# The second layer norm taken apart in a gated cross-attention block

## What is computed

```python
x1 = x + tanh(g_xattn) * attention(layernorm(x), ctx)
out = x1 + tanh(g_ffn) * ffn(layernorm(x1))

# attention, one of 8 samples, C = 256 rows by D = 1024
t = Wt @ ctx ; p = Wp @ layernorm(x) ; g = Wg @ ctx
att = sum over a group of 32 rows of p * g          # 8 groups
y = Wz (grouped) @ (att * t)
y normed over its group, * gn_w + gn_b, + ctx

# ffn, per row s of x1 after its layer norm
scores = (h @ Wq.T) @ keys.T                        # 64 experts
gate = softmax over the 16 highest scores
z = h @ A_w.T                                       # 64 experts of rank 8
out = (z * gate) @ B_w.T * 2
```

## Time and profile before

| quantity | value |
|---|---|
| device time, median of 3 runs | 394.64 us (394.6 to 395.23) |
| span of the profiled execution | 392.9 us |
| PE busy | 367.8 us, 94% of the span |
| DVE busy | 293.8 us, 75% |
| ACT busy | 131.0 us, 33% |
| POOL busy | 96.8 us, 25% |

### The profile page before, as it was taken

How to read it: one execution, slowest core, us unless ns; L and a number is a source line. 1 busy time by engine, 2 the same in 40 slices (tenths; PEclk the granted TensorE clock), 3 DMA queues, 4 the chain that set the end, 5 groups by cost and what they waited for, 6 DMA issues and landing times.

```text
span 392.9 us, 5668 instructions
## 1 busy us (share of the span) xinstructions
PE 367.8 (94%) x2051; PEld 321.2 (82%) x2051; DVE 293.8 (75%) x729; ACT 131.0 (33%) x204; POOL 96.8 (25%) x73
## 2 busy tenths in 40 slices
PE   6998489999999989999899989999899989999996
PEld 5776479888898878888798878988798878988994
DVE  3867899459974899649985799739985699738742
ACT  4574435203542136113432036213342035321310
POOL 0172152205140152304240150402440150401000
PEclk9999789999999999999999999999999999999999
DMA  7648001401150020501141011501132011001102
GB/s 257 237 139 300 15 2 44 172 0 54 53 214 0 12 95 6 207 0 53 53 160 54 0 53 53 214 0 53 53 100 113 0 53 53 0 0 53 55 24 84
DMA packets 10665, 30.36 MB, mean 77 GB/s; under 512 B 1937, under 2 KB 2705, under 8 KB 10657
## 3 DMA queue, kind: packets, MB, share of 16 engines
q1 hardware_dynamic: 10544, 30.19, 20.5%
q10 hardware_dynamic: 112, 0.07, 0.1%
HBM read 21.86 MB, written 8.39 MB: 77 GB/s over the span
## 4 chain that ended last, share of the span: by engine, by line
PE 77%; DVE 7%; POOL 6%; ACT 4%; issue 2%; DMA 2%; SPq 1%; ACTq 0%; POOLq 0%; DVEq 0%
PE w_ps L829 32%; PE z_ps L884 19%; PE w_ps L905 18%; DVE ln_sb L651 5%; POOL c_lo L294 4%; PE t_ps L870 4%; DMA x_sb<-in_x 2%; ACT c_hi L366 2%; PE t_ps L895 2%; PE w_ps L884 2%; POOL w_rs L316 1%; ACT hT_hi L396 1%; PE t_ps L812 1%; DVE x_st L501 1%; ACT q_hi L371 0%
## 5 line engine op out<-in xcount | busy, mean ns | idle before, releaser
L884 PE MATMUL z_ps<-A_hi,hT_hi 128*128 128x288 f32 x240 | 53.4, 304 | 0.6 <-DVE hT_lo L557 0.6
L884 PE MATMUL z_ps<-A_hi,hT_lo 128*128 128x288 f32 x240 | 51.9, 298 | 0.0
L884 PE MATMUL z_ps<-A_lo,hT_hi 128*128 128x288 f32 x240 | 51.9, 298 | 0.0
L905 PE MATMUL w_ps<-B_hi,zT_hi 128*128 128x512 f32 x128 | 51.3, 400 | 0.0
L304 POOL TENSOR_TENSOR q_lo<-ln_sb,q_hi 128x1024 fp32r<-128x1024 f32 x16 | 38.1, 2404 | 53.5 <-ACT q_hi L371 53.5
L905 PE MATMUL w_ps<-B_lo,zT_hi 128*128 128x512 f32 x128 | 49.9, 390 | 0.0
L905 PE MATMUL w_ps<-B_hi,zT_lo 128*128 128x512 f32 x128 | 49.9, 390 | 0.0
L396 ACT ACTIVATE hT_hi<-t_ps 128x512 fp32r<-128x512 f32 x32 | 17.4, 591 | 78.0 <-PE t_ps L870 78.0
L884 PEld LDWEIGHTS z_ps<-A_hi,hT_hi 128*128 128x128 f32 x240 | 39.4, 192 | 1.6 <-DVE hT_lo L557 1.0
L294 POOL TENSOR_TENSOR c_lo<-c_sb,c_hi 128x1024 fp32r<-128x1024 f32 x14 | 33.3, 2381 | 28.9 <-ACT c_hi L366 28.9
L884 PEld LDWEIGHTS z_ps<-A_lo,hT_hi 128*128 128x128 f32 x240 | 39.2, 192 | 0.0
(11 more groups left out here) (131 smaller groups left out, 787.8 us busy)
## 6 DMA issues: line engine op xcount, KB each, us to landing
x_sb<-in_x SPq DMA_DIRECT2D x8, 1024.0 KB, 5.0
c_sb<-in_ctx SPq DMA_DIRECT2D x7, 1024.0 KB, 7.0
out_block<-o_sb SPq DMA_DIRECT2D x14, 512.0 KB, 2.6
res_sb<-in_L_ffn_B_w SPq DMA_DIRECT2D x3, 512.0 KB, 3.5
c_sb<-in_ctx SPq DMA_DIRECT2D x2, 512.0 KB, 5.9
stage<-in_L_ffn_A_w SPq DMA_DIRECT2D x2, 512.0 KB, 6.3
res_sb<-in_L_ffn_A_w SPq DMA_DIRECT2D x2, 512.0 KB, 9.9
out_block<-o_sb SPq DMA_DIRECT2D x4, 256.0 KB, 2.0
```

The lines of the kernel that those rows point to most:

```text
L884: last = pe.matmul(banks[i][:, 0:ZH], h[:, t, row], w[:, k, i * ZH:(i + 1) * ZH], start=(k == 0 and h is hT_hi and w is A_hi), stop=(k == ...
L905: last = pe.matmul(w_ps[k][:, :], z[:, t, row], w[:, j, cols], start=(j == 0 and z is zT_hi and w is B_hi), stop=(j == KN - 1 and z is zT_lo))
```

## The change

The layer norm is split into a centring and a scale, and they go to different places:

- DVE takes the statistics of `u` from PSUM (`u_statistics(t)`), and forms minus the mean, `neg_u`. ACT waits for it (`u_mean`) and adds it as it copies `u` out of PSUM.
- `xt` is also given mean zero: DVE's instruction writes the row's sum beside it (`xt_sum`), POOL forms `neg_xt` and adds it to both tiles (`xt_center`, three instructions on POOL). For the first sample ACT makes the sums by two copies.
- So `w = u*slope + xt` has mean zero as it stands. PE transposes it from `uw_sb` without a norm. `h_tile` and the statistics of w go; ACT squares each tile with a sum beside it (`w_square`), POOL adds eps and takes the power (`w_root`, two instructions on POOL for both tiles).
- The scale `w_rs` is applied to the scores (as they leave PSUM) and to the gate (`g_scale`, one small instruction more in each `gate`).
- The residual's shift is replaced by `kappa`, made from `u_dev`, `slope` and `kappa0`; `kappa0` needs `xt_mid`, POOL's end of `xt_center`, and stands in `group_deviation`.
- Orders: `hT(1)` moves from the middle of `z_product(0)` into `out_product(3)`, and `hT(0)` into `out_product(2)`. The passes with the low part of ctx come last in a product, so that `u_product_next` waits for `c_lo` only ahead of its fifth pass. On POOL `x_root` stands ahead of `ctx_low(1)`. On DVE `x_plus_ctx` follows `x_stats` at once.

```diff
             def load(b, n_prev):
-                sp.wait_ge(xt_done, n_prev)
+                sp.wait_ge(xt_summed, n_prev)
+                sp.wait_ge(q_done[T - 1], n_prev)
...
+            def xt_center(n):
+                pool.wait_ge(xt_summed, n)
+                pool.tensor_tensor(neg_xt[:, :], xt_sum[:, :], minus_mean[:, :], ALU.mult).then_inc(pool_step, 1)
+                pool.wait_ge(pool_step, 1)
+                for t in range(T):
+                    last = pool.tensor_scalar(xt_sb[:, t, :], xt_sb[:, t, :], 1.0, neg_xt[:, t:t + 1],
+                                              ALU.mult, ALU.add)
+                last.then_inc(xt_mid, 1)
+
+            def w_root(n):
+                pool.wait_ge(w_squared, T * n if isinstance(n, int) else pool_w_squared)
+                pool.tensor_tensor(w_ve[:, :], w_sq[:, :], eps[:, :], ALU.add).then_inc(pool_step, 1)
+                pool.wait_ge(pool_step, 2)
+                pool.tensor_tensor(w_rs[:, :], w_ve[:, :], minus_half[:, :], ALU.pow).then_inc(w_rstd, 1)
...
+            def w_square(t, n):
+                act.wait_ge(w_done[t], n)
+                act.wait_ge(p_done[USES - 1], n)
+                act.activation(q_hi[:, t, :], uw_sb[:, t, :], ACT.Square, scale=1.0 / math.sqrt(D),
+                               accum_out=w_sq[:, t:t + 1]).then_inc(w_squared, 1)
...
                 act.wait_ge(u_done[k], n)
-                act.activation(uw_sb[:, t, h * HALF:(h + 1) * HALF], w_ps[k][:, :], ACT.Copy).then_inc(u_copied[k], 1)
+                act.wait_ge(u_mean[t], n)
+                act.activation(uw_sb[:, t, h * HALF:(h + 1) * HALF], w_ps[k][:, :], ACT.Identity,
+                               bias=neg_u[:, t:t + 1]).then_inc(u_copied[k], 1)
...
             for k in range(USES):
-                u_copy(k, 1)
                 for n in groups_after_u(k):
                     prep(n)
+                if k % NH == NH - 1:
+                    for j in range(k - NH + 1, k + 1):
+                        u_copy(j, 1)
                 if k == 1:
                     query_hi(1)
...
+            act.wait_ge(xt_done, 1)
+            for t in range(T):
+                last = act.activation(hT_hi[:, t, :], xt_sb[:, t, :], ACT.Copy, accum_out=xt_sum[:, t:t + 1])
+            last.then_inc(xt_summed, 1)
             for n in range(n_late, len(PREP)):
                 prep(n)
...
+            def u_statistics(t, n):
+                for h in range(NH):
+                    k = NH * t + h
+                    dve.wait_ge(u_done[k], n)
+                    step(dve.bn_stats(u_st[:, t, 6 * h:6 * h + 6], w_ps[k][:, :]))
+                settle()
+                step(dve.bn_aggr(u_mv[:, t, :], u_st[:, t, :]))
+                settle()
+                dve.tensor_scalar(neg_u[:, t:t + 1], u_mv[:, t, 0:1], -1.0, None, ALU.mult).then_inc(u_mean[t], 1)
...
                 step(dve.tensor_tensor(att_var[:, T:2 * T], a2[:, :], u_mv[:, :, 1], ALU.add))
+                dve.wait_ge(xt_mid, n)
+                step(dve.tensor_tensor(kappa0[:, :], gnb_t[:, :], neg_xt[:, :], ALU.subtract))
...
             def ffn_and_next(n, m, n_dma, m_dma):
                 x_stats(m, m_dma)
-                hT_low(1, n)
+                x_plus_ctx(m, m_dma)
                 gate(0, n)
+                u_statistics(0, m)
                 query(m, n)
-                x_plus_ctx(m, m_dma)
-                u_statistics(m)
+                u_statistics(1, m)
                 zT_low(0, n)
...
-                passes = [(w, v, c) for c in range(T) for w, v in ((w_hi, v_hi), (w_hi, v_lo), (w_lo, v_hi))]
+                passes = [(w, v_hi, c) for c in range(T) for w in (w_hi, w_lo)] + [(w_hi, v_lo, c) for c in range(T)]
...
-                out_product(2, n)
-                pe.wait_ge(zT_lo_s[1], n)
-                hT(0, m)
+                out_product(2, n, lambda: hT(0, m))
                 pe.wait_ge(p_reduced[3], m)
-                out_product(3, n)
+                out_product(3, n, lambda: hT(1, m))
```

More of the change, by code:

```diff
@@ L111, in flamingo_block @@
         y_ve, y_rs = sb("y_ve", [P, T]), sb("y_rs", [P, T])
-        slope, shift = sb("slope", [P, T]), sb("shift", [P, T])
+        slope, kappa = sb("slope", [P, T]), sb("kappa", [P, T])
         sc, sc1, sc2 = sb("sc", [P, NE]), sb("sc1", [P, NE]), sb("sc2", [P, NE])
@@ L440, in ffn_and_next @@
                 residual(n)
-                hT_high(1, n)
                 exps(0, n)
+                act.wait_ge(hT_done[2 * T - 1], n)
                 act.wait_ge(res_done, n)
-                for k in range(USES):
+                for k in range(NH):
+                    u_copy(k, m)
+                query_hi(m)
+                for k in range(NH, USES):
                     u_copy(k, m)
                 zT_high(0, n)
-                query_hi(m)
                 exps(1, n)
@@ L452, in ffn_and_next @@
                         zT_high(1, n)
-                hT_high(0, m)
+                for t in range(T):
+                    w_square(t, m)
+                    hT_high(t, m)
             with act.Fori(0, NB - 1) as b:
@@ L639, in shifts, with w_tile @@
-            def shifts():
-                step(dve.tensor_tensor(shift[:, :], g_mean[:, :], slope[:, :], ALU.mult))
-                settle()
-                step(dve.tensor_tensor(shift[:, :], gnb_t[:, :], shift[:, :], ALU.subtract))
-            def h_tile(t, n):
-                dve.wait_ge(w_rstd[t], n)
-                dve.wait_ge(q_lo_s, n)
-                for h in range(NH):
-                    cols = slice(h * HALF, (h + 1) * HALF)
-                    dve.tensor_scalar(ln_sb[:, t, cols], uw_sb[:, t, cols], w_mv[:, t, 0:1], w_rs[:, t:t + 1],
-                                      ALU.subtract, ALU.mult).then_inc(h_done[NH * t + h], 1)
+            def w_tile(t, n):
+                for k in range(NH * t, NH * t + NH):
+                    dve.wait_ge(u_copied[k], n)
+                dve.scalar_tensor_tensor(uw_sb[:, t, :], uw_sb[:, t, :], slope[:, t:t + 1], xt_sb[:, t, :],
+                                         ALU.mult, ALU.add).then_inc(w_done[t], 1)
@@ L654, in finish_attention, with offsets @@
+            def offsets():
+                step(dve.tensor_tensor(kappa[:, :], u_dev[:, :], slope[:, :], ALU.mult))
+                settle()
+                dve.tensor_tensor(kappa[:, :], kappa[:, :], kappa0[:, :], ALU.add).then_inc(kappa_done, 1)
             def finish_attention(n, add=lambda k: None):
                 slopes(n)
-                w_tile(0)
-                shifts()
+                for t in range(T):
+                    w_tile(t, n)
+                offsets()
                 add(0)
-                h_tile(0, n)
@@ L661, in finish_attention @@
                 add(1)
-                w_tile(1, lambda g: hT_low_part(0, g, n))
+                hT_low(0, n)
                 add(2)
-                h_tile(1, n)
+                hT_low(1, n)
                 add(3)
@@ L705, in _ @@
                     query(1, None)
-            for n in groups_after_pg(0, 0):
-                prep(n)
-            def second_group():
-                for n in groups_after_pg(0, 1):
+                if k == NH - 1:
+                    u_statistics(0, 1)
+            u_statistics(T - 1, 1)
+            for i in range(2):
+                for n in groups_after_pg(0, i):
                     prep(n)
-            u_statistics(1, second_group)
             dve.wait_ge(gn_in, 32)
@@ L832, in u_product_first, with lows @@
             def u_product_first(between):
-                pe.wait_ge(c_lo_first, 1)
+                def lows(c):
+                    pe.wait_ge(c_lo_first if c == 0 else c_lo_s, 1)
+                pe.wait_ge(prep_lo, SMALL.index("wu") + 1)
+                for t in range(T):
+                    pe.wait_ge(c_hi_s[t], 1)
                 for k in range(USES):
-                    product(w_ps[k][:, :], Wu_hi, Wu_lo, c_hi, c_lo, k, u_done[k],
-                            (lambda: pe.wait_ge(c_lo_s, 1)) if k == 0 else None)
+                    product(w_ps[k][:, :], Wu_hi, Wu_lo, c_hi, c_lo, k, u_done[k], lows if k == 0 else None)
                     between(k)
@@ L938, in _ @@
                 prep(n)
-            hT(0, 1)
+            for t in range(T):
+                hT(t, 1)
             def ffn_and_next(n, m):
-                def second_tile():
-                    pe.wait_ge(hT_lo_s[0], n)
-                    hT(1, n)
-                z_product(0, n, second_tile)
+                z_product(0, n)
                 u_product_next(n, m)
```

106 lines of the change are left out of this document (47 added, 59 removed).

## The result

| | before | changed |
|---|---|---|
| device time, median | 394.62 us (394.45 to 395.23) | 403.02 us (401.17 to 403.36) |
| span of the profiled execution | 392.9 us | 401.4 us |
| DVE busy | 293.8 us | 251.9 us |
| ACT busy | 131.0 us | 151.7 us |
| POOL busy | 96.8 us | 125.0 us |

The ratio is 1.0193, 95% interval 1.0167 to 1.0219. The forecast was 411.1, with 391.8 to 414.0 as its range: the right sign, but 16.5 us more where 8.4 came. DVE lost 42 us of work, and the kernel became slower.

A forecast was written before the change was run, and what follows sets the result against it. PE, busy 94% of the span, was taken as the bound. Span 392.9 + 11.2 (first body) + 1.5 (clock) + 3.6 (six bodies) + 0.2 (tail) = 409.4; with 1.74 to device time, 411.1 us; range 391.8 to 414.

The forecast's parts named there:

- the mechanism and the places: Loop: waits at `hT` go; DVE's `x_plus_ctx` holds POOL's `x_rs`, so PE waits 2.5 us for `c_lo` at u's fifth pass.
- the two waits of the first stage: First stage: `q_hi` behind copies of u and `neg_u`, 18.02 to 22.2; DVE's last reduction behind `xt_mid`, 37.30 to 49.1.
- The relief of PE: Loop on PE: `hT(1)` moves into `out_product(3)`, so u's start comes 1.90 us earlier per body.
- The clock: First body: half clock behind PE's wait of some 4.4 us costs 0 or 3.0 us; 1.5 taken.
- the price of the wait in the loop: PE's wait for `c_lo` at u's fifth pass, 2.5 us a body; with the -1.90, +0.6 a body.
- the serial sum of `x_rs` and DVE's second instruction: Loop: `x_rs` waits for `x_plus_ctx`'s first instruction, the second for `x_rs`, then `c_lo` for the second, ending at 194.6.
- the first stage: Ahead of the loop: new waits on ACT, POOL and DVE shift the first body's u by 11.2 us.
- ACT's part: First stage on ACT: `q_hi` at 22.2 instead of 18.02, the last `B_hi` at 40.7 instead of 35.83.
- The tail: End of the kernel: `g_scale` lengthens the gate ahead of `zT(0)`, +0.2 us.
- (1): Rival: no exclusion between `x_plus_ctx` and POOL; first shift 8.8, each body 1.8 us faster, device time 392.8; chance 0.25.
- (2): Rival: POOL goes on at once behind DVE's first instruction; shift 10.0, -0.7 a body, device time 400.6; chance 0.22.
- (3): Rival: first stage 3 us cheaper in each case, because ACT's queue is not last to be ready; no separate chance given.

The follow-up runs named there:

- e4b: The changed kernel with POOL's second `c_lo` moved between `w_root` and `x_root`: 399.1 us, ratio 1.0102 to the kernel before.

## Why the prediction was right or wrong

**Right: the mechanism and the places.** The waits at `hT` went and PE waits for `c_lo` in all seven bodies; DVE's pair holds `x_rs` and `c_lo`, for which no row of before had an example; the sign; the two waits of the first stage. The relief of PE, -1.90 a body, was measured at -1.82. The clock, 1.5 us, was right in size by luck: it was the middle between two ends, 0 and 3.0, and measured was neither. Half clock did come, behind a shorter wait, 3.1 us and not 4.4, and for 3 us of the product instead of 6.

**Wrong: the price of the wait in the loop**, 2.5 us, where u grew by 1.35. The failed step is the serial sum of `x_rs` and DVE's second instruction: "Then `x_rs` waits until 190.2 and ends at 190.9. If DVE's second instruction, which by then waits, goes next, it ends at 192.2 and `c_lo` at 194.6". From DVE's start to the end of `c_lo` this is 5.8 us; measured are 158.3 - 153.6 = 4.7. `x_rs` holds nobody, although it is an instruction of 0.70 us. I had read off how long a large instruction holds, and let a small one hold as long. Six bodies at -0.35 instead of +0.6 make 5.7 of the 8.0 us between the forecast span (409.4) and the measured one (401.4).

**Wrong in size: the first stage**, a shift of 8.5 us where I said 11.2; that is 2.7 us more. ACT's part came even later than said, `q_hi` by 0.5 (22.68) and the last `B_hi` by 0.9 (41.59). An `xt_center` took 1.1 us, between the bounds 0.9 and 2.36 and below the 1.6 that I took by the select of the earlier trace rows; with it the last reduction started at 48.15, not 49.1, and `w_tile` at 51.46, not 52.3. From there to `x_ve`, which lets `x_rs` go, went 11.5 us (62.91), forecast 12.4 (64.7). From `x_ve` to the end of `c_lo` went 4.8 us, forecast 5.7, by the step of the loop once more. So the error has three parts of 0.8 to 1.0 us each, none of them the largest by much.

**The tail**: 0.5 instead of 0.2 us, 0.3 of it the gate and 0.1 the last u behind its wait.

**The rivals.** (1), no exclusion, fell with `x_rs` at 1.66. (2), 400.6, was nearer to the time (403.0) than my forecast, for a reason of its own: its -0.7 a body assumed that POOL's `c_lo` goes in between DVE's two, which the changed kernel does not do and e4b does. I said the point of decision was whether `x_rs` can run inside `x_plus_ctx`. It decides between exclusion and none, but what priced the exclusion was that DVE's second instruction can run beside the 0.7 us of `x_rs`. (3), a first stage 3 us cheaper, came true in size (2.7) and not for its reason, since ACT's part was late and not early. The range held the time.
